# Three layers on one Trainium2 core: where the opening folds the first attention's weights, and which engine takes the weights' remainders

## The reference, cut to what matters

```
x = x + 0.5 * _L0_ffn_ref(_layernorm(x), expert_sel, keys, values)        # layer 1
x = x + _L0_attn_ref(_layernorm(x), Wq, bq, Wk, bk, Wv, bv, Wo, bo, projection)   # layer 2
...                                                                        # four more layers

def _L0_ffn_ref(x, expert_sel, keys, values):      # 32 experts of 64 hidden numbers, 4 chosen per token
    gates = sigmoid(xt @ expert_sel.T)
    sel_val, sel_idx = top_k(gates, 4);  gate_full = zeros.at[sel_idx].set(sel_val)
    scores = relu(einsum('nd,edf->nef', xt, keys)) * gate_full[:, :, None]
    return einsum('nef,efv->nv', scores, values)

def _L0_attn_ref(x, ...):                          # 16 heads of 8, 32 features each
    Q, K, V = heads(x @ Wq + bq), heads(x @ Wk + bk), heads(x @ Wv + bv)
    Qp, Kp = (relu(einsum('bhsd,hfd->bhsf', t / norm(t), projection)) + 0.1 for t in (Q, K))
    ...
```

## Time and profile before

| | us |
|---|---|
| median of 3 runs | 1649.67 |
| lowest, highest | 1648.46, 1650.84 |
| the profiled execution, its own time | 1646.87 |
| its span in the trace | 1645.1 |
| TensorE busy | 1442.1 (88%) |
| VectorE busy | 1345.3 (82%) |
| ScalarE busy | 1026.5 (62%) |
| GpSimd busy | 856.8 (52%) |

### The profile page before, as it was taken

The page is one execution under the profiler, slowest core; times in us unless marked ns, Lnnn a source line. Parts: engine busy times, 40 slices in busy tenths (PEclk is TensorE's granted clock), DMA queues, the critical chain, the costliest instruction groups (busy, mean ns, idle before and its releaser), DMA issues.

```text
span 1645.1 us, 28122 instructions
## 1 busy us (share of the span) xinstructions
PE 1442.1 (88%) x8269; PEld 1095.3 (67%) x8269; DVE 1345.3 (82%) x3897; ACT 1026.5 (62%) x2300; POOL 856.8 (52%) x745
## 2 busy tenths in 40 slices
PE   5999998997999995999639999999999899779991
PEld 4777877654666663999527666666666666459880
DVE  7599998666667776888779999999999867768887
ACT  7544442365323233889668999999999723259880
POOL 5856662210133334467646666666666215537772
PEclk9999998999999997999869999999999999879995
DMA  9992001000011103222199900000000001122225
GB/s 196 179 177 34 1 6 48 1 1 1 26 33 33 45 19 89 60 74 74 49 212 181 163 1 1 2 1 1 1 1 2 1 14 36 43 56 74 72 59 153
DMA packets 156499, 91.24 MB, mean 55 GB/s; under 512 B 19414, under 2 KB 151207, under 8 KB 156353
## 3 DMA queue, kind: packets, MB, share of 16 engines
q1 hardware_dynamic: 142464, 70.52, 22.3%
q0 software_dynamic: 9664, 16.89, 3.2%
q10 hardware_dynamic: 4224, 2.10, 0.4%
HBM read 31.93 MB, written 60.53 MB: 56 GB/s over the span
## 4 chain that ended last, share of the span: by engine, by line
PE 55%; issue 12%; DVE 12%; POOL 10%; ACT 8%; DMA 2%; POOLq 0%; SPq 0%; DVEq 0%; ACTq 0%
PE psum L1379 9%; POOL answers L2443 8%; PE psum L2829 8%; PE psum L2854 5%; PE psum L661 5%; PE psum L662 4%; PE psum L663 4%; ACT psum L2935 4%; DVE psum L2955 3%; PE psum L2807 2%; PE psum L2808 2%; PE psum L2809 2%; PE psum L1134 1%; PE psum L1136 1%; PE psum L1135 1%
## 5 line engine op out<-in xcount | busy, mean ns | idle before, releaser
L2935 ACT ACTIVATE psum<-psum,gate 128x128 f32<-128x128 f32 (+7 forms) x512 | 368.6, 729 | 33.2 <-DVE gate L2955 31.5
L2955 DVE CUSTOM_DVE_ANT_0 psum<-psum,cmask 128x128 f32<-128x128 f32 (+7 forms) x512 | 371.0, 791 | 12.7 <-PE psum L2829 11.4
L1379 PE MATMUL psum<-raw_all,w 128*128 128x512 f32 x384 | 195.4, 592 | 1.5 <-DVE raw_all L1522 1.5
L661 PE MATMUL psum<-xl,wreg 128*128 128x512 f32 x320 | 181.6, 567 | 2.8 <-ACT psum L2935 1.5
L1520 DVE SCALAR_TENSOR_TENSOR raw_all<-psum,hg 128x512 f32<-128x512 f32 x128 | 88.1, 690 | 57.3 <-PE psum L663 55.2
L662 PE MATMUL psum<-xh,wreg 128*128 128x512 f32 x320 | 126.9, 397 | 0.0
L663 PE MATMUL psum<-xh,wreg 128*128 128x512 f32 x320 | 126.7, 396 | 0.0
L2829 PE MATMUL psum<-hh,hl 64*128 64x384 f32 (+3 forms) x768 | 114.4, 373 | 12.7 <-ACT psum L2935 12.7
L2829 PE MATMUL psum<-spare_sets_room 64*128 64x384 f32 (+3 forms) x768 | 114.0, 369 | 12.3 <-ACT psum L2935 12.3
L2443 POOL DMA_INDIRECT answers<-ed,xl x90 | 99.9, 1109 | 31.1 <-issue 30.8
L2829 PEld LDWEIGHTS psum<-hh,hl 64*128 64x128 f32 x768 | 86.3, 190 | 40.7 <-ACT psum L2935 33.7
(11 more groups left out here) (440 smaller groups left out, 4220.9 us busy)
## 6 DMA issues: line engine op xcount, KB each, us to landing
rows<-blank SPq DMA_DIRECT2D x146, 258.0 KB, 6.7
xl<-rows SPq DMA_DIRECT2D x58, 193.5 KB
raw_all<-answers SPq DMA_DIRECT2D x32, 256.0 KB, 4.1
w<-in_L_ffn_W_dram SPq DMA_DIRECT2D x16, 256.0 KB
x<-in_L_attn_x_dram SPq DMA_DIRECT2D x4, 512.0 KB, 5.6
out_dram<-x ACTq DMA_DIRECT2D x8, 256.0 KB, 4.1
answers<-ed,xl POOLq DMA_INDIRECT x90
answers<-row,xl POOLq DMA_INDIRECT x84
```

Of the source, the lines that this page charges most:

```text
L661: pe.matmul(dst, wh, xl[:, blk(i)], start=start, stop=False)
L1379: pe.matmul(bank(B_OUT[i % 2]), col(dn, j), hidden[:, n % HID, :], start=(j == 0), stop=(j == nf - 1)).then_inc(S["dn_done"], 1)
L2935: return act.activation(src, src, ACT.Exp, bias=kept_at(arg, u, q, a), scale=-1.0, accum_out=kept_at(esum, u, q, a))
L2955: return dve.tensor_tensor_reduce(src, src, mask, 1.0, 3e38, ALU.add, ALU.min, kept_at(arg, u, q, a))
```

## The change

The four folds leave the end of the opening and go into block 0 of the first network: TensorE's parts after up products 0, 1, 2 and 4, ScalarE's copies after `hh` of the same tiles. Fold 2 goes to another bank (5) and waits for two earlier readers of it (`a_hi`, `centred`). What the folds read and write gets a room of its own (`fold_room`), so that the wait for `raw_read` goes. GpSimd's late work goes into block 0 too: the `xl` of blocks 6 and 7 after tiles 3 and 5, the attention matrices' remainders after tile 7, the folded matrices' after tiles 9 and 11. Of the four quarters of the down weights' remainders GpSimd keeps two and VectorE does two, after its last `choose` of the opening. The first down product waits for GpSimd's quarters (`rest_done` 3), the ninth for VectorE's (`rest_dve`), the first of block 1 for `folds_out`.

```diff
+    fold_room = sb("fold_room", [P, 4 * BLK], F32, setup_mem)
-    turned_w, b_cols, pbd = raw_flat[:, 0:2 * P], raw_flat[:, 2 * P:3 * P], raw_flat[:, BLK:2 * BLK]
-    raw_fold = raw_flat[:, 2 * BLK:4 * BLK].rearrange("p (k n) -> p k n", k=2)
+    turned_w, b_cols, pbd = fold_room[:, 0:2 * P], fold_room[:, 2 * P:3 * P], fold_room[:, BLK:2 * BLK]
+    raw_fold = fold_room[:, 2 * BLK:4 * BLK].rearrange("p (k n) -> p k n", k=2)
...
-            for i in range(NB):
-                low(i)
+            for i in range(LOWS_FIRST):                      # LOWS_FIRST = HALF + 2
+                low(pool, i)
                 if i >= HALF:
                     for part in range(2):
-                        last = rest_of(i // 2 - 2, i % 2 * 2 + part, 4)
+                        last = rest_of(pool, 0, (i - HALF) * 2 + part, 4)
                     last.then_inc(S["rest_done"], 1)
-            rest_of(2, 0, 1)
-            for k, w in enumerate((wkp, wqp)):
+            for part in range(2):
+                last = rest_of(pool, 1, part, 4)
+            last.then_inc(S["rest_done"], 1)
...
+        def late_pool(pool, j):
+            if j in (3, 5):
+                low(pool, LOWS_FIRST + (j - 3) // 2)
+            if j == 7:
+                rest_of(pool, 2, 0, 1)
+            if j in (9, 11):
+                k = (j - 9) // 2
                 pool.wait_ge(fold_raw, k + 1)
                 pool.wait_ge(fold_out, k + 1)
+                w = (wkp, wqp)[k]
                 pool.tensor_tensor(w[:, 1], raw_fold[:, k, :], w[:, 0].bitcast(F32), ALU.subtract).then_inc(S["raw_read"], 1)
+
+        FOLD_AT = {0: 0, 1: 1, 2: 2, 4: 3}
+
+        def late_pe(pe, j):
+            if j not in FOLD_AT:
+                return
+            k = FOLD_AT[j]
+            if k < 2:
+                pe.wait_ge(wp_out, 3)
+                pe.matmul(bank((B_V, B_W)[k]), turned_w[:, k * P:(k + 1) * P], pbd, start=True, stop=True).then_inc(folded, 1)
+            elif k == 2:
+                pe.wait_ge(a_hi, 1)
+                pe.wait_ge(S["centred"], 1)
+                pe.matmul(bank(B_M), b_cols, pbd, start=True, stop=True).then_inc(folded, 1)
...
         def tensor(pe):
...
-                if i >= 7:
-                    for k in range(2):
-                        fold(2 * (i - 7) + k)
...
         def scalar(act):
...
-            for k in range(4):
-                fold(k)
...
-            dve.tensor_tensor(wg_centred[:], rawG[:], bank(B_M)[:, BLK // 2:BLK // 2 + E1], ALU.subtract)
+            dve.tensor_tensor(wg_centred[:], rawG[:], bank(B_M)[:, BLK // 2:BLK // 2 + E1], ALU.subtract).then_inc(S["centred"], 1)
+            for part in range(2, 4):
+                last = rest_of(dve, 1, part, 4)
+            last.then_inc(S["rest_dve"], 1)
...
                 if n == 0:
-                    pe.wait_ge(ahead["rest_done"], NB // 2)
+                    pe.wait_ge(ahead["rest_done"], 3)
+                    pe.wait_ge(ahead["wp_out"], 1)
+                if n == nf // 2:
+                    pe.wait_ge(ahead["rest_dve"], 1)
+                if n == nf:
                     pe.wait_ge(ahead["folds_out"], 1)
...
                     if i == 0 and j == 0:
                         gates_of(0)
+                    if i == 0:
+                        folds.tensor(pe, j)
...
-                if n == 2:
-                    act.wait_ge(ahead["raw_read"], 2)
                 act.activation(hh[:, j % SLOTS, :], kept[n % len(kept)], ACT.Copy).then_inc(S["hi_done"], 1)
...
                     if live:
                         high(i, j, at == 0)
+                    if i == 0:
+                        folds.scalar(act, j)
...
                     if live and not by_dve(j):
                         low(i, j, at == 0)
+                    if i == 0:
+                        folds.gpsimd(pool, j)
```

More of the change, by code:

```diff
@@ L84 @@
     next: object
+@dataclass
+class Folds:
+    tensor: Callable
+    scalar: Callable
+    gpsimd: Callable
 @dataclass
@@ L364, in setup @@
         names = ("measured", "step", "set", "xn_ready", "xT_done", "xT_out", "xh_done", "filled", "logit_done", "gate_in", "max_done",
[L365 removed]
+                 "top_set", "rest_set", "gate_set", "rest_done", "folds_out", "raw_read", "xT_read", "rest_dve", "centred")
         S = {n: sem("op_" + n) for n in names}
         zeroed = sem("zeroed")
[L368 removed]
+        S["consts"], S["wp_out"] = consts, wp_out
         NLOAD = 13
@@ L450, in gpsimd @@
             pool.tensor_copy(iota[0:1, 0:1], iota[0:1, 0:1]).then_inc(consts, 1)
[L452 to L462, removed]
@@ new lines, in gpsimd, with low, rest_of @@
+            last.then_inc(S["rest_done"], 1)
+        LOWS_FIRST = HALF + 2
+        def low(pool, i):
+            pool.wait_ge(S["xT_out"], i + 1)
+            pool.wait_ge(S["xh_done"], i + 1)
+            pool.tensor_tensor(xl[:, blk(i)], xT[:, blk(i)], xh[:, blk(i)].bitcast(F32), ALU.subtract).then_inc(S["xT_read"], 1)
+        def rest_of(e, k, part, parts):
+            hi, lo, w = weights[k]
+            e.wait_ge(cast, k + 1)
+            step = w.shape[1] // parts
+            some = slice(part * step, (part + 1) * step)
+            return e.tensor_tensor(lo[:, some], w[:, some], hi[:, some].bitcast(F32), ALU.subtract)
@@ new lines, in late_pe @@
+        def late_pe(pe, j):
[9 more added lines that the diff above has]
+                pe.matmul(bank(B_M), b_cols, pbd, start=True, stop=True).then_inc(folded, 1)
+            else:
+                pe.wait_ge(fold_out, 1)
+                for c in range(NCH):
+                    last = pe.matmul(bank(B_V)[:, c:c + 1], pbd[:, c * P:(c + 1) * P], bcol[:, 0:1], start=True, stop=True)
+                last.then_inc(folded, 1)
@@ new lines, in late_act @@
+        def late_act(act, j):
+            if j not in FOLD_AT:
+                return
+            k = FOLD_AT[j]
+            act.wait_ge(folded, k + 1)
+            if k < 2:
+                src = bank((B_V, B_W)[k])
+                act.activation(raw_fold[:, k, :], src, ACT.Copy).then_inc(fold_raw, 1)
+                act.activation((wkp, wqp)[k][:, 0], src, ACT.Copy).then_inc(fold_out, 1)
+            elif k == 2:
+                act.activation(neg_bp[:], bank(B_M), ACT.Copy, scale=-1.0)
+                for c in range(NCH):
+                    mine = slice(c * KVW, (c + 1) * KVW)
+                    act.activation(bp_rows[mine, :], bank(B_M)[mine, c * P:(c + 1) * P], ACT.Copy)
+                    act.activation(mask4[mine, :], headones[mine, :].rearrange("p (h d) -> p h d", d=HD0)
+                                   [:, c * HPC:(c + 1) * HPC, 0], ACT.Copy)
+            else:
+                act.activation(bp_cols[:], bank(B_V)[:, 0:NCH], ACT.Copy).then_inc(S["folds_out"], 1)
@@ L504, in small_ones @@
                 pe.matmul(bank(B_M)[:, BLK // 2:BLK // 2 + E1], mean_of[:], rawG[:], start=True, stop=True).then_inc(tr_done, 1)
[L506 to L516, removed]
             pe.wait_ge(consts, 1)
@@ L566, in little_ones @@
                 act.activation(bias_of[:, :, F1 // P], bank(B_M)[:, NF1:NF1 + E1], ACT.Copy).then_inc(a_hi, 1)
[L568 to L582, removed]
             act.wait_ge(s_turned, 1)
@@ L1011, in moe_low, with gated @@
                            ).then_inc(M["split"], 1)
-    def gated(ph, ahead, choose_late, nf, up, dn, scale):
+    def gated(ph, ahead, choose_late, folds, nf, up, dn, scale):
         names = ["up_done", "g_done", "g_copied", "hg_done", "hi_done", "lo_dve", "lo_pool", "dn_done", "oT_ready",
@@ L3000, in program @@
     def program():
-        opening, choose_late = setup()
-        ffn_1, late = gated("f0", opening.S, choose_late, dn=(f_dnh, f_dnl), **ffn)
+        opening, choose_late, folds = setup()
+        ffn_1, late = gated("f0", opening.S, choose_late, folds, dn=(f_dnh, f_dnl), **ffn)
         keys, end_pe, end_dve = linear_kv(ffn_1.S, late)
```

2 lines of the change are left out of this document (1 added, 1 removed).

## The result

The changed kernel takes 1656.87 us (median of 8 runs, 1654.22 to 1664.57) against 1647.68 for the kernel before beside it (8 runs, 1643.49 to 1651.79). The ratio is 1.0062, 95% interval [1.0042, 1.0082]: slower by 7 to 13.5 us, where I had forecast no change. The profiled execution took 1657.46, its span is 1655.7 (before 1645.1).

A forecast was written before the change was run, and what follows sets the result against it. TensorE was taken to bound the opening's chain and block 0. Clock -2.8, gap -0.26, start +0.2 and GpSimd +2.8 gave -0.06, rounded -0.1: 1649.6 us against the median 1649.67, range 1646.2 to 1652.9.

The forecast's parts named there:

- Start: First up product of block 0: starts at 43.8 in place of 50.53; last logits' wait costs TensorE 0.2 us.
- Clock: TensorE, opening into block 0: clock rises at 48.8 (47.7 to 49.9) in place of 54.4, gaining 2.8 us (2.25 to 3.35).
- Gap at the first down product: Block 0: TensorE's 0.26 us gap before the first down product goes, because GpSimd's work is ready; 0.26 us gained.
- Backlog: Block 0: GpSimd's late work makes TensorE wait 1.7 and 1.1 us, 2.8 lost; 0.7 without VectorE and GpSimd excluding each other.
- that rival: Block 0: TensorE's pauses at down products 8 and 12 make its clock fall, +3.8 us, 1653.4; chance 0.13.
- The one in which the change doesn't bring the clock: Start of block 0: clock rise waits until 54.4 as before, +2.4 us, 1652.1; chance 0.1.
- VectorE's half: Before block 0's first gate: VectorE's two remainder instructions end by 46.7, costing nothing, or 0.3 us if pieces collide worse.
- The sum of block 0: Clock -2.8, gap -0.26, start +0.2, GpSimd +2.8 give -0.06 us, bounds -2.7 to +2.7.
- what is won or lost there should arrive at the end of the kernel unchanged: After block 0: everything is relative to its end, so its gain or loss reaches the kernel's end unchanged.
- The other moves cost nothing: Remaining moves: no transfer issued or moved past, new room holds no live network data, `raw_read` wait had ended; no cost.
- my rivals: Three: GpSimd's backlog never reaches TensorE (1646.2, chance 0.14); pauses cost the clock (1653.4, 0.13); no earlier clock (1652.1, 0.1).

The follow-up runs named there:

- 4 fills more: The kernel before with 4 tiny VectorE fills added in its idle time of the opening: 1649.14 us, one run (before beside it 1646.24).
- two fewer: The changed kernel with the opening's three VectorE fills of the gates' rooms written as one: 1649.26 us, ratio 1.0011 to the kernel before.
- guarded: The changed kernel with GpSimd waiting for VectorE's last placing step ahead of the next expert's two weight remainders: 1636.5 us, ratio 1.0003 to the kernel before.
- 128 fills more: The kernel before with 128 tiny VectorE fills added in its idle time of the opening: 1640.82 us, one run (before beside it 1636.77).
- the block 2 version: The changed kernel, three fills in one, GpSimd's late work spread over blocks 0 and 2: 1645.0 us, ratio 0.9998 to the kernel before.
- two added fills: The kernel before with the opening's three VectorE fills of the gates' rooms written as five: 1658.95 us, ratio 1.0053 to the kernel before.

## Why the prediction was wrong

*Start.* Forecast 43.8, measured 43.95. Held.

*Clock.* Forecast 48.8, bounds 47.7 and 49.9; it rose inside 46.2 to 47.0, outside the bounds, so that against the profile of before the term is some (54.4 - 46.6) / 2 = 3.9 in place of 2.8. But that the moved folds bring the early rise is not shown. TensorE in the two kernels with VectorE's half alone and with 4 fills more, which both leave the folds in the opening:

```profile
49.85 0.40 PE L669 MATMUL psum<-xh,wreg 128*128 128x512 f32 x1
50.09 0.39 PE L670 MATMUL psum<-xh,wreg 128*128 128x512 f32 x1
```
```profile
49.38 0.39 PE L665 MATMUL psum<-xh,wreg 128*128 128x512 f32 x1
49.60 0.39 PE L666 MATMUL psum<-xh,wreg 128*128 128x512 f32 x1
```

These are the L662 and L663 of before. With steps of 0.24 and 0.22 they are at the high level in their first up product, at a time when the kernel before stood at the lower one for 4 us more. By the traces' clock records, which the granted-clock column is made from, the high level begins between 46.8 and 49.9 us in the seven kernels with moved folds. In the seven with the folds in the opening it begins between 54.3 and 55.1 in four, at 52.6 in one (where it was high from 45.7 to 49.2 too), and by 46.8 and 46.1 in these two. The prediction took the one late rise of its single profile for a property of the order of work.

*Gap at the first down product.* It is gone. Clock, gap, start and whatever else comes ahead of it can be read together: that product starts at 52.69 in place of 56.63, 3.94 us earlier, and my terms had 2.86.

*Backlog.* Forecast 2.8 us, with waits beginning at 64.5 and 72.0. TensorE waited 1.10 us until 65.22 and 0.45 until 71.83, and the lead shrank from 3.94 to 1.56: 2.4 in all. By its beginnings (64.1, 71.4) the account of GpSimd's work was right. The same account gave 0.7 without exclusion of VectorE and GpSimd, and 2.4 is near the value with it. By the Trainium skill (SBUF — State Buffer, "Who interferes with whom") a VectorE instruction with two inputs in SBUF and a GpSimd one that reads SBUF exclude each other on a shared port; the trace agrees, with two of GpSimd's pieces, 1.29 us elsewhere, that take 1.76 and 1.75 (59.41 and 66.30) beside VectorE's own remainders (58.93 and 65.79). The pauses didn't cost the clock in block 0 (granted 1.00 from 60 to 83 us): that rival fell. The one in which the change doesn't bring the clock can't be called fallen, for the reason above.

*VectorE's half.* Forecast to end by 46.7 and cost nothing where it stands. It ran 44.13 to 46.42, the first gate began at 47.17 where I had 46.8. Held, for the work. But the two instructions move every later one of VectorE on by two places, and that cost the 9 us.

*The sum of block 0.* Forecast -0.06, bounds -2.7 and +2.7; measured -1.56, inside; with a rise that moves by more than 8 us between executions, that is in part luck. The medians of the kernels without long comparison (1.0011 [0.9995, 1.0027] with two fewer, 1.0003 [0.9987, 1.0019] guarded) don't show even this, and the traces say why: in those of three kernels whose folds stayed in the opening (the half alone, 4 and 128 fills more) block 0 also ends 1.2 to 1.8 us ahead of the kernel before's. The 1.56 can come from the moment at which the clock rose in these two executions alone; whether anything of it is the change's stays open. Later on the same holds: the block 2 version's profiled span is 6.7 us below that of before, its ratio 0.9998.

*The step that failed* is the sentence in the first part: "what is won or lost there should arrive at the end of the kernel unchanged". With it went "The other moves cost nothing", since I costed VectorE's two instructions by duration alone. What took its place: 0.35 us of late start at 495 us, a short comparison that now had to wait for two remainders, two pauses of 3.11 us, and the lower clock behind each. By the matched starts of TensorE's instructions the kernel after is 4.4 us ahead before the first, 2.0 behind once its clock is back, 6.8 behind after the second: 6.4 + 4.8 = 11.2 us, exactly what two added fills gave. The clock's part of it is 11.2 - 2 x 3.11 = 5.0; the granted clocks of the four rows above say the same, 10 x (0.09 + 0.25 + 0.12 + 0.05) = 5.1, with 1.00 in the kernel before until 626. The end of the span is 10.6 us later. The seven kernels with the long comparison absent have ratios of 0.9984 to 1.0015, the three timed with it 1.0053 to 1.0062, and no interval of one kind overlaps one of the other.

Could it have been seen ahead of time? Not the 128. But the near tie was in the trace of before: 0.78 us behind the comparison's start GpSimd begins 2.5 us of remainders, and TensorE waits for the comparison; at 444.94 us a collision of this kind had already cost it 1.60 us. None of the rows that the prediction rests on lies behind 320 us, and a case "a near tie later on turns the other way" was among none of my rivals.

## What to carry to other kernels

Before a small edit, look for near ties on the critical path in the whole trace, not only where the edit is: a short VectorE instruction that TensorE waits for, close ahead of long GpSimd work on SBUF, is one, and a semaphore that puts the GpSimd work behind it makes the kernel robust against it (here it took back the whole 0.6%, 1.6 us of it by a collision that the kernel before had too). When a time moves by more than the edited stage did, match the two traces instruction by instruction and find the first jump. Before a gain is put down to a clock that rises earlier, see when it rises in several executions of the unchanged order. To tell the work of an added instruction from its place in the program, add as many trivial ones instead.

## What the runs showed of the hardware

A VectorE instruction that waits starts 0.35 us later than otherwise (0.44 in place of 0.09 us behind its semaphore) at some of the places that repeat with 128 in VectorE's list. The profile's queue of instruction loads suggests why, as the page of the kernel after has it (packets, MB, share):

```profile
q14 instruction: 80, 0.66, 0.1%
```

These are 8.2 KB a packet. The Trainium skill (Runtime: NRT & Kernel Launch, "Instruction fetch mechanics") has 256 instructions in 16 KiB, so by its size of an instruction a packet is an estimated 128 of them; it calls the cost of a crossing mostly hidden, and here 0.35 us is seen where the instruction waits anyway. The times fit: in the changed kernel packets of this queue start at 496.04 and 618.60, 0.66 and 0.93 us behind the two late instructions. That the loading is the cause is argued from sizes and times, not shown.

A VectorE comparison of 0.30 us took 3.1, the length of two GpSimd instructions in a row and more, though its record begins 0.42 to 0.47 us ahead of the first of them (eight cases in four kernels); at 0.76 us or more it took 0.30. So a record's start doesn't say which of the two goes first. Where between 0.47 and 0.76 the turn is, no run shows. These comparisons ended only behind both remainders, but that isn't so everywhere: at 444.94 us of the kernel before the short step that began inside the first remainder (444.45 to 445.73) ended at 445.77, between the two, and only the next one (445.81 to 447.00) waited for the second (until 446.95).
